# First attention of a fused four-layer kernel: another place in the iteration for the weighted sums and for three of the maximum and score tiles

## What is computed

```python
x = layer_norm(x, ln_m_g, ln_m_b)        # the context, (4, 32, 128)
lat = layer_norm(latents, ln_l_g, ln_l_b)  # x normalised, (4, 512, 128)
q = lat @ Wq
kv = jnp.concatenate([x, lat], axis=1) @ Wkv
k, v = jnp.split(kv, 2, axis=-1)
q, k, v = (split_heads(q), split_heads(k), split_heads(v))   # 16 heads of 64
dots = jnp.einsum('bhid,bhjd->bhij', q, k) * scale
attn = jax.nn.softmax(dots, axis=-1)
out = jnp.einsum('bhij,bhjd->bhid', attn, v)
return out.transpose(0, 2, 1, 3).reshape(b, m, heads * dim_head) @ Wout
```

## Time and profile before

| | us |
|---|---|
| median of 3 runs | 792.94 |
| lowest and highest run | 791.82, 796.18 |
| span of the profiled execution | 798.2 |
| PE busy in the span | 713.8 |
| DVE busy | 491.6 |
| ACT busy | 366.9 |
| POOL busy | 378.2 |

### The profile page before, as it was taken

One profiled execution on the slowest core, in us unless ns is written; L12 is line 12 of the kernel. 1 busy time (PEld: TensorE's weight loads), 2 busy tenths in 40 slices (PEclk: granted clock), 3 DMA queues, 4 the chain that ended last, 5 costly groups with the idle time before them and its releaser, 6 DMA issues.

```text
span 798.2 us, 13900 instructions
## 1 busy us (share of the span) xinstructions
PE 713.8 (89%) x4626; PEld 414.0 (52%) x4626; DVE 491.6 (62%) x1077; ACT 366.9 (46%) x572; POOL 378.2 (47%) x369
## 2 busy tenths in 40 slices
PE   4899999999999999999999999987995587659991
PEld 4655556545556545555545455454664244326660
DVE  4655484595594875675775666664442477746673
ACT  5465554564654553654554643432332543314440
POOL 6254453553563573464375454524222314765552
PEclk9999999999999999999999999999998688569996
DMA  9999999300000000000030004302111500122224
GB/s 235 163 161 160 158 160 157 43 1 1 1 2 1 6 10 1 1 1 2 1 119 1 1 1 106 119 18 58 36 39 56 174 2 28 37 72 67 81 69 177
DMA packets 69132, 50.45 MB, mean 63 GB/s; under 512 B 4068, under 2 KB 62312, under 8 KB 69064
## 3 DMA queue, kind: packets, MB, share of 16 engines
q1 hardware_dynamic: 65544, 42.30, 29.7%
q0 software_dynamic: 3520, 7.27, 2.8%
HBM read 20.07 MB, written 29.47 MB: 62 GB/s over the span
## 4 chain that ended last, share of the span: by engine, by line
PE 75%; DVE 8%; issue 6%; POOL 4%; ACT 3%; DMA 2%; another core or an unknown queue 1%; SPq 1%; DVEq 0%; POOLq 0%; ACTq 0%
PE PSUM L1602 14%; PE PSUM L1634 13%; PE PSUM L1444 7%; PE PSUM L1569 5%; PE PSUM L1469 4%; PE PSUM L1700 4%; PE PSUM L1403 4%; PE PSUM L1407 3%; PE PSUM L1409 2%; PE PSUM L1408 2%; PE PSUM L1583 2%; PE PSUM L1576 2%; PE PSUM L1620 2%; PE PSUM L1664 2%; POOL results_d L643 2%
## 5 line engine op out<-in xcount | busy, mean ns | idle before, releaser
L838 ACT ACTIVATE PT<-PSUM 128x1024 f32<-128x1024 f32 x128 | 128.7, 1025 | 134.2 <-PE PSUM L1602 133.9
L671 POOL TENSOR_TENSOR PSUMS<-PT 128x1024 f32<-128x1024 f32 x32 | 76.1, 2378 | 210.6 <-ACT PT L838 171.6
L671 POOL TENSOR_TENSOR PSUMS<-PSUMS,PT 128x1024 f32<-128x1024 f32 x62 | 149.7, 2415 | 16.6 <-ACT PT L838 9.7
L1235 DVE TENSOR_REDUCE TOPS<-PSUM 128x2 f32<-128x1024 f32 x128 | 152.0, 1220 | 7.4 <-PE PSUM L1569 7.0
L1634 PE MATMUL PSUM<-PT,BIG 128*64 128x512 f32 x512 | 130.6, 611 | 0.6 <-issue 0.6
L1444 PE MATMUL PSUM<-BIG,XGT 128*128 x170 | 86.5, 614 | 2.4 <-issue 1.6
L1225 DVE TENSOR_TENSOR KL<-PSUM,KH 128x512 fp32r<-128x512 f32 x32 | 22.1, 692 | 68.0 <-ACT KH L816 67.5
L1189 DVE TENSOR_TENSOR SIL<-SIL,PSUM 128x256 f32<-128x256 f32 (+1 forms) x62 | 32.1, 518 | 48.0 <-ACT SIL L758 45.4
L1569 PE MATMUL PSUM<-KH,QH 64*128 64x512 f32 x256 | 58.0, 449 | 3.9 <-DVE QL L1228 3.6
L1634 PEld LDWEIGHTS PSUM<-PT,BIG 128*64 128x64 f32 x512 | 28.4, 135 | 54.0 <-issue 52.5
L1602 PE MATMUL PSUM<-QH,KH 64*128 64x512 f32 x256 | 54.9, 424 | 1.0 <-DVE QL L1228 0.8
(11 more groups left out here) (255 smaller groups left out, 1358.5 us busy)
## 6 DMA issues: line engine op xcount, KB each, us to landing
lists_d<-EMPTY SPq DMA_DIRECT2D x3, 2730.0 KB, 44.7
lists_b<-EMPTY SPq DMA_DIRECT2D x3, 2470.0 KB, 41.7
lists_d<-EMPTY SPq DMA_DIRECT2D x1, 2665.0 KB, 43.9
XG<-lists_d SPq DMA_DIRECT2D x39, 65.0 KB
lists_b<-EMPTY SPq DMA_DIRECT2D x1, 2405.0 KB, 20.6
BIG<-in_L_ffn_w SPq DMA_DIRECT2D x1, 2048.0 KB
W2ALL<-in_L_ffn_w SPq DMA_DIRECT2D x4, 512.0 KB, 6.1
PT<-results_d SPq DMA_DIRECT2D x8, 256.0 KB, 4.9
```

Of the source, the lines that this page charges most:

```text
L671: pool.tensor_tensor(PSUMS[:, i % 2], PTT[:, i % 2, 0] if kt == 1 else PSUMS[:, i % 2], PTT[:, i % 2, kt], ALU.add).then_inc(s_ps, 1)
L838: act.activation(PTT[:, i % 2, kt], PSUM[:, place:place + 2, :], ACT.Exp, scale=DH ** -0.5).then_inc(s_exp, 1)
L1235: dve.tensor_reduce(TOPS[:, c, 0, :], PSUM[:, place:place + 2, :], AX.X, ALU.max).then_inc(s_max, 1)
```

## The change

One line of the hand-written order. The third weighted sum (p2) moves from ahead of the third top tile (t2) to behind it, so that it stands together with p3, and both stand ahead of the fourth top tile (t3). The step at D and the second score tile (s1) move from behind t2 to ahead of it. The third score tile (s2) moves from behind the context's top tile (t4), P0 and P2, to ahead of t4; s3 stays behind them.

```diff
         ITERATION = (
-            "E A B PC CA0 C CA1 O0 ADD CS V qk p0 p1 t0 s0 t1 p2 t2 D s1 t3 p3 t4 P0 P2 s2 s3 rows mt O1 OUT "
+            "E A B PC CA0 C CA1 O0 ADD CS V qk p0 p1 t0 s0 t1 D s1 t2 p2 p3 t3 s2 t4 P0 P2 s3 rows mt O1 OUT "
             "O2 O3").split()
```

## The result

| | before | after |
|---|---|---|
| median, us | 792.59 | 817.31 |
| lowest and highest of 4 runs | 791.82, 796.18 | 816.31, 818.73 |
| ratio, with 95% interval | | 1.0298 (1.0272 to 1.0324) |
| span of the profiled execution | 798.2 | 816.4 |
| loop, from the second pair's t0 to the last mt | 463.8 | 488.2 |

The account below looks back on a forecast made before the run. PE was taken to bound the loop. Plain iterations 8.2, late ones 4.0 and those with P0 and P2 2.7 sum to 14.9, less 0.3 for the last: 14.6 more, 807.5 us, range 802 to 812.

Parts of the forecast that it names:

- PE bounds the loop, and a wait of PE is new time: Loop over head pairs: PE busy 454.7 of 460 us, so any added wait for another engine lengthens the time.
- s1 waits for t0's maximum, 0.43; t2 at 2.93: Second score tile waits 0.43 us for the first top tile's PSUM pair; t2 starts 2.93 after t0.
- s3 waits for t3's maximum, 0.18; mt at 8.13: Last score tile waits 0.18 us for t3's PSUM pair; the turn of the maxima starts 8.13 after t0.
- fewer than 40: Sign in PE's wait list: fewer than 40 waits for the maxima would mean a wrong working at s1's release.
- Plain iterations 0.43, late ones 0.80: Loop: 19 plain iterations cost 0.43 us more each, five where DVE finishes the queries' low part late 0.80 each.
- 6 x 0.45 = 2.7: Six iterations that also spread the reciprocals (P0, P2) cost some 0.45 us more each, 2.7 together.
- GpSimd's and the DMA queue's lists do not change: Instruction lists of GpSimd and the DMA queue stay as before; no cost was entered for them.
- The first iteration, and the stretch behind: First iteration, with value tiles for sums, put at 0 (bound 0.3 either way); the stretch behind the loop only shifts.
- The gain without the waits: Rival: s1 and s3 find their pairs free, only the 0.25 saved per iteration shows; 8 less, 785 us; chance 0.05.
- The array hides the waits: Rival: 0.16 of each PE wait passes while the former tile drains; 793, or up to 797 us; chance 0.07.
- DVE becomes the bound: Rival: every iteration behaves like the late ones, 30 x 0.80 = 24 more, 817 us; chance 0.06.
- The clock: Rival: the granted clock falls in the loop; at 0.79, 121 us would come on top; chance 0.02.

Follow-up runs that it names:

- experiment 2: Kernel before with only the third score tile (s2) moved ahead of t4, P0 and P2; 813.53 us, ratio 1.0153.
- experiment 11: Changed kernel with one operand of line 1261 in PSUM and the maxima of t0 to t3 taken over half their keys; 811.59 us, ratio 1.008.
- experiment 3: Changed kernel with one operand of line 1261 (the reciprocals) in PSUM; 817.19 us, ratio 1.0234.
- experiment 1: Kernel before with p2 and p3 together behind t2, D and s1 ahead of t2, and s2 left behind P2; 824.38 us, ratio 1.0326.
- experiment 7: Kernel before with p2 and p3 together but ahead of t2, s1 still behind t2, and s2 behind P2; 811.40 us, ratio 1.0234.
- experiment 4: Kernel before with one operand of line 1261 in PSUM; 800.43 us against 799.66, ratio 1.0009.
- experiment 8: Kernel before with line 1261's operand in PSUM and the first quarter of the reciprocals moved behind mt; 791.11 us against 793.24, ratio 0.9972.
- experiment 12: Kernel before with line 1261's operand in PSUM and the maxima of t0 to t3 over half their keys; 803.23 us, ratio 0.9974.
- experiment 5: Changed kernel run again, unaltered, on another group's chip; 817.90 us, ratio 1.031.

## Why the prediction was right, and where it failed

- **PE bounds the loop, and a wait of PE is new time.** Right: the loop's 24.4 are the medians' 24.7.
- **s1 waits for t0's maximum, 0.43; t2 at 2.93.** Right to 0.01. Experiments 2 and 11 show it from both sides: with s1 in its old place, or with shorter maxima, the wait is gone.
- **s3 waits for t3's maximum, 0.18; mt at 8.13.** Right within 0.05. It hardly shows in the list of waits (24 entries at L1602, all of them at s1, not the 60 that I asked for), as the former tile's busy time of 0.39 for a slot of 0.23 covers it. I had written that 0.16 of each wait would not be printed and then counted entries all the same. By my own bound, fewer than 40, the working would be wrong; the starts of the tiles show that the bound was.
- **Plain iterations 0.43, late ones 0.80.** 0.48 and 0.85 (0.62 for pair 30). Small in size.
- **"6 x 0.45 = 2.7" for the iterations with P0 and P2.** This term failed: it is 11.7 for seven, against 3.5 with pair 31's 0.80. Experiment 3, where line 1261 is not held, has 3.7 for the seven: 0.5 in pairs 7, 15 and 23, near the working's 0.45, 0.8 in 11, 19 and 27, and -0.17 in 31. The other 8.0, over two thirds, is line 1261 with what follows from it.
- **"GpSimd's and the DMA queue's lists do not change."** True of the lists, and the step at which the forecast failed: it was taken to mean that nothing changes there, so the length of DVE's own instructions beside GpSimd's additions was put at no change without a reason. Measured, that is 7.9 of the 24.4 us. The times of the additions against DVE did change, by 0.75 for the additions and 0.6 for the joined maximum, and the two engines exclude each other at line 1261. The profile before had shown it: line 1261 at 1.06, and at 0.69 where no addition ran. I read the durations of DVE in a plain iteration, which holds no such instruction.
- **Pair 17.** It was counted as plain and costs 1.95, and 2.36 and 1.94 in experiments 1 and 3, so not by line 1261. Ahead of it two of DVE's small steps of the router's ranking are each held by an addition:

```profile
279.57 1.45 DVE L1057 TENSOR_TENSOR PLACE<-ROUT,PLACE 128x32 f32<-128x32 f32 x1
...
281.27 2.23 DVE L1061 CAST SLOT<-RSM 128x4 int32<-128x4 f32 x1
```

  Before, the first took 0.16 and only the cast 2.39, and QL was there in time. It is the same failed step, with another instruction: the first one, a product of two operands in SBUF, now meets an addition that it just missed. The other runs bear this out. Where the product is held (2.05 in experiment 1, 1.62 in experiment 2), the pair costs 2.36 and 1.56; in experiment 7 it takes 0.25, and the pair costs 0.44 like a plain one. Experiment 2 leaves D where it was, so the move of D is not needed for it. No run has this product with an operand in PSUM.
- **The first iteration, and the stretch behind.** 0 was forecast for the first and -0.54 measured, outside my bound of 0.3. It need not be the change: the kernel before with other edits has -0.64, -0.63 and -0.86 there (experiments 4, 8 and 12), so the profile of before is the odd one. The stretch behind was to shift only; it is 9 us shorter, of which the clock can explain at most 7.
- **The gain without the waits** did not come. Experiment 11 gives it what it asked for, s1 at 1.51, and finds 0.03, since s0's exponential is next: **the 8 us of this rival left out a wait**. In the change itself t2 starts at 2.93, behind that exponential, and the 0.25 stand in the sum as the prediction has them. The loop of experiment 11 is still 2.7 longer than before's.
- **The array hides the waits:** no, 0.43 stands in the starts. **DVE becomes the bound:** its 817 is what was measured, but not by that way; 17 iterations behave as plain ones, and DVE was not busier but held.
- **The clock.** 1.00 over the loop, and the waits of 0.25 printed in nearly every iteration leave it there. But after the pair of long waits (1.19 and 0.63) at pair 19 it falls to 1.2 GHz for 3.4 us:

```profile
313.00:316.50 3.50, 1.78 (x12) 0.91 (x12) 3.47 (x5) 1.03 (x2) 0.44 (x1) 1.00 0.00 0
316.50:320.00 3.50, 3.41 (x14) 1.69 (x16) 2.30 (x2) 1.02 (x1) 0.00 (x0) 0.62 0.00 0
```

  (columns as in the first fence). There p2 and p3 take 3.06 busy for 1.94, and pair 19 costs 3.92 where pair 11 costs 2.29: 1.6 us, once. Experiments 2 and 5 have two such falls, at pairs 11 and 19, in experiment 2 after a single wait of 1.54 us; the other traces have none in the loop. At pair 27 the same waits stand in all three profiles, and the clock stays. So 1.6 of the 7.9 and 3.1 of the 10.1 is clock, given away by line 1261's hold. The rule of the Trainium skill that the prediction named would have the short, regular waits bring the clock down; in no trace here did they.

The parts do not add: an early s2 alone costs the loop 13.3, the sums together 19.1, both 24.4. With the operand in PSUM they are 3.2 and, for both, 16.5, so of the 24.4 the hold of line 1261 is 7.9, and by experiment 11 the waits for the maxima are 13.8. The 2.7 that are left are pair 17 (1.4 in experiment 11) and six iterations with P0 and P2 (2.3 together, PE waiting there for an exponential), less what other pairs gain.

## What to carry to other kernels

A weighted sum that takes no PSUM bank is cover for the release of the others: whoever moves it must count, for each tile, the work left between it and the last use of its pair. When a change shifts two engines against each other by a few tenths, look for DVE instructions with two operands in SBUF, and for casts, beside GpSimd instructions, read their duration in every instance (one that differs between instances of the same shape is held), and put one of two operands into PSUM where that is possible. And look at starts, not at printed idle time, where a matmul's busy time is longer than its slot.

## What the runs showed of the hardware

- A DVE subtraction of 64x512 with both operands in SBUF takes 0.69 us alone and up to 2.58 beside a GpSimd addition of 128x1024 (2.39), and ends 0.54 or 0.55 us behind the addition wherever it is held; with one operand in PSUM it takes 0.68 or 0.69 always. If DVE holds first, the addition is the one that gets longer (2.66 in before, up to 2.88 in experiment 1).
- The same holds for tiny ones: a cast of 128x4, with one operand, takes 0.17 or 2.39, a 128x32 product 0.16 or 1.45.
- The reciprocals beside them, with one SBUF operand, never changed (0.88 to 0.95 in 28 instances of before and of after), nor did the maxima out of PSUM (1.22).
- The granted clock fell to 1.2 GHz for 3.4 us in the loop five times: three times in the change's two profiles after PE waits of 1.2 and 0.6 us close together, twice in experiment 2 after one of 1.54. It did not fall at pair 27 after the same waits; what decides is open.
